# A four-layer attention and expert kernel: statistics taken where rows are made, a new order of matmuls in the second self attention

## The reference

```python
x = x + L0_xattn(ctx, layernorm(x), mask, ...)   # queries: x. keys: x and ctx. 8 heads of width 64
x = x + L0_ffn(layernorm(x), Wg, W1, W2)         # experts, one for each row
x = x + L1_xattn(layernorm(x), ctx, ctx, ...)    # 16 heads, softmax over 77 context rows, with wo
x = x + L1_ffn(layernorm(x), ...)                # self attention with 16 heads of 16, then 8 experts, 2 a row
x = x + L2_xattn(layernorm(x), ctx, pair_mask)   # 16 heads, relu squared over its sum, with wo
x = x + L2_ffn(layernorm(x), ...)                # 8 experts, 2 a row
x = x + L3_xattn(layernorm(x), ctx, ...)         # 16 heads, softmax, no wo
x = x + L3_ffn(layernorm(x), ...)                # fp4 rounded gate, up and down
```

```python
scores = einsum('bqhd,bkhd->bhqk', q, k) / sqrt(16)      # 2 x 16 heads x 1024 x 1024
o = einsum('bhqk,bkhd->bqhd', softmax(scores), v)
```

## Time and profile before

| | |
|---|---|
| median of 3 runs | 2685.7 us (2677.44 to 2688.1) |
| the profiled execution | 2695.88 us, its span 2694.1 us |
| PE busy with matmuls | 2201.1 us (82%) |
| PE busy with weight loads | 1304.1 us (48%) |
| DVE | 1298.8 us (48%) |
| ACT | 1087.3 us (40%) |
| POOL | 651.7 us (24%) |
| moved by DMA | 214.34 MB, mean 80 GB/s |
| instructions | 36343 |

### The profile page before, as it was taken

How to read it: one execution, slowest core, us unless ns; L and a number is a source line. 1 busy time by engine, 2 the same in 40 slices (tenths; PEclk the granted TensorE clock), 3 DMA queues, 4 the chain that set the end, 5 groups by cost and what they waited for, 6 DMA issues and landing times. The chain is left out here.

```text
span 2694.1 us, 36343 instructions
## 1 busy us (share of the span) xinstructions
PE 2201.1 (82%) x12198; PEld 1304.1 (48%) x12199; DVE 1298.8 (48%) x2560; ACT 1087.3 (40%) x2189; POOL 651.7 (24%) x569
## 2 busy tenths in 40 slices
PE   5899999953948766999998399994976999767786
PEld 2333333242933431333333299994345999633454
DVE  5655555165154557578871600004452350164785
ACT  3434444420314511566666244442532444325111
POOL 1238888911520050000000022220001222110011
PEclk9899999985977885699999699997887999978898
DMA  2000000022610053223420665652036666400000
GB/s 64 5 1 13 13 10 13 25 67 91 203 59 1 20 148 40 32 32 45 51 33 1 190 214 195 199 191 89 1 118 233 198 201 203 138 13 1 0 1 32
DMA packets 141630, 214.34 MB, mean 80 GB/s; under 512 B 39600, under 2 KB 97644, under 8 KB 141500
## 3 DMA queue, kind: packets, MB, share of 16 engines
q1 hardware_dynamic: 131228, 186.10, 25.3%
q0 software_dynamic: 9696, 26.49, 2.6%
q10 hardware_dynamic: 576, 0.07, 0.0%
HBM read 182.00 MB, written 30.15 MB: 79 GB/s over the span
## 5 line engine op out<-in xcount | busy, mean ns | idle before, releaser
L1840 DVE TENSOR_REDUCE heads_part_max<-heads_shared_ps 128x2 f32<-128x1024 f32 x256 | 300.1, 1220 | 93.5 <-PE heads_shared_ps L1757 93.5
L1824 ACT ACTIVATE heads_probs<-heads_score_ps 128x512 f32<-128x512 f32 x512 | 266.4, 603 | 194.4 <-PE heads_score_ps L1779 194.4
L2873 PE MATMUL experts_up_ps<-experts_rowT,experts_w 128*128 128x128 f32 x2864 | 342.9, 279 | 0.0
L2873 PEld LDWEIGHTS experts_up_ps<-experts_rowT,experts_w 128*128 128x128 f32 x2864 | 334.9, 195 | 0.2
L3033 DVE TENSOR_TENSOR experts_y<-experts_down_ps,experts_b_now 128x256 f32<-128x256 f32 x78 | 33.1, 425 | 499.5 <-PE experts_down_ps L2883 499.3
L1354 POOL TENSOR_TENSOR core_xT<-core_xT,heads_probs 128x1024 f32<-128x1024 f32 (+1 forms) x112 | 264.4, 2360 | 24.0 <-ACT heads_probs L1527 10.5
L2941 ACT ACTIVATE experts_hT<-experts_up_ps,experts_b_now 128x128 f32<-128x128 f32 x624 | 222.8, 367 | 49.0 <-PE experts_up_ps L2873 11.8
L1566 DVE TENSOR_REDUCE heads_part_max<-heads_shared_ps 128x1 f32<-128x512 f32 x256 | 164.5, 686 | 146.7 <-PE heads_shared_ps L1396 146.5
L1779 PE MATMUL heads_score_ps<-heads_q,heads_k 66*128 66x512 f32 x512 | 199.4, 478 | 29.2 <-ACT heads_probs L1824 24.9
L2822 POOL DMA_INDIRECT y_dram<-experts_y,experts_index x101 | 99.4, 984 | 456.3 <-DVE experts_y L3033 412.0
L1527 ACT ACTIVATE heads_probs<-heads_score_ps 128x1024 f32<-128x1024 f32 x128 | 131.0, 1023 | 177.8 <-PE heads_score_ps L1423 177.8
(11 more groups left out here) (557 smaller groups left out, 3242.7 us busy)
## 6 DMA issues: line engine op xcount, KB each, us to landing
experts_w<-in_L_ffn_W SPq DMA_DIRECT2D x39, 1024.0 KB, 5.2
experts_w<-in_L_ffn_w SPq DMA_DIRECT2D x39, 1024.0 KB, 5.0
experts_w<-in_L_ffn_W SPq DMA_DIRECT2D x23, 512.0 KB, 4.0
experts_w<-y_dram SPq DMA_DIRECT2D x20, 512.0 KB, 4.7
experts_b_now<-in_L_ffn_b SPq DMA_DIRECT2D x78, 128.0 KB, 2.9
heads_q<-l_queries SPq DMA_DIRECT2D x32, 256.0 KB, 11.9
heads_k<-l_keys SPq DMA_DIRECT2D x32, 256.0 KB, 13.6
l1f_w<-in_L_ffn_W SPq DMA_DIRECT2D x8, 1024.0 KB, 10.6
```

Source lines behind the costliest of these rows:

```text
L1824: act.activation(probs[:, t % SLOTS_OF_PROBS, r, :], score_ps[:, i % RING, :], ACT.Exp, scale=SC).then_inc(exp_done, 1)
L1840: dve.tensor_reduce(part_max[:, g % 2, 2 * pair:2 * pair + 2, s, x], two, AX.X, ALU.max).then_inc(shared_read, 1)
L2873: done = pe.matmul(up_ps[:, f % 4, 0:SLOT], w1_sb[:, u, c, f * P:(f + 1) * P], rowT[:, u % 2, c, :], start=(c == 0), stop=(c == DC - 1))
```

## The change

Three things change.

1. **Statistics.** `core.stats` is a new buffer of the whole program (128 x 16 x 6). Whoever makes rows also takes their `bn_stats` into it: the load (now in four DMAs of four tiles, with a semaphore each), the last adds of heads0, x1, x2, x3 and out1, and the combine of the experts. `layer_norm` no longer takes any. It works in one piece of 16 tiles, not in two of eight, and ACT takes the root of one column (`warm`) ahead of all else in the stage. The rows of the experts come back into four buffers (in the space of `w1`, as before), so SP no longer waits for `combined` between them.
2. **Queries** of x1 and x3: the four matmuls for `m + 2` stand behind jobs 1, 2, 3 and 4 of `m`, one each, not all behind job 7.
3. **Second self attention.** The fourth score of a step stands behind the step's two peak items, not before them. And `keep_running(n)` is new: n full matmuls of 512 columns, whose result nobody reads, 18 ahead of step 0, and one behind each of the first three scores and of each peak item in steps 0 and 1 (10 more).

The core of the diff:

```diff
+        self.stats = stage.sb("stats", [P, NT, 6])
...
-            sp.dma_start(core.x[:], x.rearrange("b (t p) d -> p (b t) d", p=P)).then_inc(x_loaded, 16)
-            sp.wait_ge(x_loaded, 16)
+            for u in range(NT // FOUR):
+                sp.dma_start(core.x[:, FOUR * u:FOUR * (u + 1), :], tiles[:, FOUR * u:FOUR * (u + 1), :]
+                             ).then_inc(x_loaded[u], 16)
...
+            for t in range(NT):
+                if t % FOUR == 0:
+                    dve.wait_ge(x_loaded[t // FOUR], 16)
+                dve.bn_stats(core.stats[:, t, :], core.x[:, t, :]).then_inc(counted, 1)
...
-            def statistics(t):
-                dve.bn_stats(stats[:, t, :], source[:, t, :]).then_inc(stats_done, 1)
...
             dve.memset(eps[:], LN_EPS).then_inc(eps_done, 1)
-            for t in range(PER):
-                statistics(t)
...
+            done(dve.tensor_tensor(diff[:], stats[:, :, 1], stats[:, :, 4], ALU.subtract))
+            done(dve.tensor_tensor(var[:], stats[:, :, 2], stats[:, :, 5], ALU.add))
+            done(dve.tensor_tensor(mean[:], stats[:, :, 1], stats[:, :, 4], ALU.add))
...
+            dve.wait_ge(std_done, 1)
+            done(dve.reciprocal(rstd[:], std[:]))
...
+            for t in range(NT):
                 normalise(t)
...
+            act.activation(warm[:], eps[:], ACT.Sqrt).then_inc(warmed, 1)
+            act.wait_ge(var_done, 1)
+            act.activation(std[:], var[:], ACT.Sqrt, scale=1.0 / D, bias=eps[:, 0:1]).then_inc(std_done, 1)
...
                     for job in range(8 * m, 8 * (m + 1)):
                         peak(job)
-                    if m + 2 < T // 512:
-                        queries(m + 2)
+                        x = job - 8 * m
+                        if m + 2 < T // 512 and 1 <= x <= DC * DC:
+                            query(m + 2, (x - 1) // DC, (x - 1) % DC)
...
                     dve.tensor_tensor(rows, rows, heads_out[:, part, :, :], ALU.add).then_inc(added, 1)
+                    if g == DC - 1:
+                        dve.wait_ge(added, part + 1)
+                        for t in range(b * BT, (b + 1) * BT):
+                            dve.bn_stats(core.stats[:, t, :], core.x[:, t, :]).then_inc(counted, 1)
...
+                for t in range(g * GROUP, (g + 1) * GROUP):
+                    dve.wait_ge(finished, t + 1)
+                    dve.bn_stats(core.stats[:, t, :], core.x[:, t, :]).then_inc(counted, 1)
...
+        BEFORE, EARLY = 18, 2
...
+            def keep_running(times):
+                for _ in range(times):
+                    pe.matmul(sums_ps[:], q_narrow[:, 0, 0:P], q_narrow[:, 0, 0:512], start=True,
+                              stop=True).then_inc(rested, 1)
+
             for item in work_at[-1]:
                 share(item)
+            keep_running(BEFORE)
             for t in range(STEPS):
                 items = work_at[t]
-                for r in range(QUAD):
+                early = t < EARLY
+                for r in range(QUAD - 1):
                     score(t, r)
+                    if early:
+                        keep_running(1)
                 for item in items[0:2]:
                     share(item)
+                    if early:
+                        keep_running(1)
+                score(t, QUAD - 1)
+                if t == 1:
+                    pe.wait_ge(rested, BEFORE + EARLY * (QUAD + 1))
                 if t:
                     value(t - 1)
...
             for x in range(NT // TILES):
-                if x >= 2:
-                    sp.wait_ge(combined, TILES * K * (x - 1))
                 for k in range(K):
...
-                    sp.dma_start(back[:, x % 2, k, :, :], y_dram[first:first + TILES * P, :].rearrange(
-                        "(t p) d -> p t d", p=P)).then_inc(returned[x % 2], 16)
+                    sp.dma_start(back[:, x, k, :, :], y_dram[first:first + TILES * P, :].rearrange(
+                        "(t p) d -> p t d", p=P)).then_inc(returned[x], 16)
...
+                for y in range(TILES):
+                    t = x * TILES + y
+                    dve.wait_ge(combined, TILES * (K * (x + 1) - 1) + y + 1)
+                    dve.bn_stats(core.stats[:, t, :], core.x[:, t, :]).then_inc(counted, 1)
```

135 lines of the change are left out of this document (57 added, 78 removed).

## The result

The changed kernel took 2606.97 us (median of 4 runs, 2598.55 to 2609.01); the kernel before, on the same chip, 2686.9 us (4 runs). The ratio is 0.9703, with an interval of 0.9671 to 0.9735. The forecast was 2610, a ratio of 0.972, in a range of 2585 to 2642. The profiled execution of the changed kernel took 2606.4 us with a span of 2604.7; the one of before had 2694.1. That one stood about 9 us above its kernel's median, the one after at its median.

The account below looks back on a forecast made before the run. No one engine bounds the kernel: handover holes and a falling TensorE clock do. Norms with producers -29, clock -22, order -15, queries -11 sum to -77, taken as -76: 2695.9 to 2620 profiled, 2610 us as median; range 2585 to 2642.

Parts of the forecast that it names:

- Norms (-44.7): Nine layer norms: delay from first statistic to first normalised row falls from 62.6 to 20.4 us; with smaller gains, 44.7 less.
- Producers (+16): Stages that make rows pay for the statistics where DVE has no slack: combines, first self attention, x1 to x3, load; 15.8 us.
- the four buffers: Combines of sparse rows: loads all out at once land ahead, so DVE bounds; this pays a part of the statistics.
- Clock (-22): Second self attention: full matmuls raise the clock before the first score; first fifteen steps 67.8 to 43.6 us, start 2.2 later.
- the loop of DVE and two buffers: Second self attention: second peak pair needs the buffer freed by the previous step's second reduce, giving a 2.75 us step.
- the step that this would give: Second self attention: if the score waits for the whole drain and its weights, step some 2.81 us, order part -9.
- a clock that rises no earlier: Rival, second self attention: full matmuls do not raise the clock earlier; +2 in place of -22, 2634 us; chance 0.12.
- 15 x 0.45 us: Second self attention, in that rival: got back from the order over 15 steps, of 0.55 us the fourth score waits.
- Queries (-11): x1 and x3: query matmuls spread over jobs 1 to 4 make a round 8.1 us against 11.5; 11 us less.
- The lower end of the range, -25: Whole kernel: the parts' bounds taken as independent give some -25 and +32, with the first three rivals within 2585 to 2642.
- the parts' bounds: Whole kernel: margins about -6/+11 (norms and producers), -4/+24 (clock), -11/+15 (order), -2/+9 (queries) us.
- two signs of being wrong: Second self attention: steps of 4 us past the first and steps above 2.85 us would show the forecast wrong.

## Why the prediction was right, point by point

**Norms (-44.7): right**, -47.9. The first hats came at 1.46, 1.95 and 3.2 us against 1.45, 2.15 and 3.35. None waited for anything else, and no stage behind gave it back.

**Producers (+16): right**, about +16 by the stages (load 1.9, heads0 3.1, gates and experts 7.9, x3 3.5 in the run with the statistics alone). The combines cost +6.7 of +8.1, the load +1.9, the last 2.71 us of x3's statistics stand behind its last sum (forecast 2.8):

```profile
2396.71 1.23 DVE L784 TENSOR_TENSOR core_x<-core_x,x_heads_out 128x1024 f32<-128x1024 f32 x1
2397.97 2.71 DVE L788 BATCH_NORM_STATS2 core_stats<-core_x 128x6 f32<-128x256 f32 x8
```

What the text said of the four buffers, that they pay a part of the statistics, was wrong: they pay nothing. With statistics between the sums, the loads land in time in two buffers as well.

**Clock (-22): right in size**. Steps 0 to 14 took 43.5 us against 67.8 (forecast 43.6), and the first score came 1.7 us later behind the first peak item (51.5 against 49.8; forecast 2.2): -22.6. What no row had shown, how soon the clock answers, is 1.9 to 4.9 us.

**Order (-15): right in size and in mechanism**, -17.3 (41.6 less 24.3). The step was to be 2.75 in the mean by the loop of DVE and two buffers, and is 2.64 and 2.85 in turn; with less of DVE's work it falls to 2.64 and no lower, against the 2.66 forecast for a step without that loop. The Trainium skill (TensorEngine Tiling (Array Packing), Key Properties) has it that a change of the tiling mode drains TensorE; the step that this would give was put at 2.81. In the changed kernel the fourth change stands where PE used to wait, and the step is 2.64 where DVE does not hold it, 0.03 over the 2.61 of a step without peaks. The rule is not refuted by that: with PE full and one change more (the second item behind the values), a step took 0.31 more, of which some 0.10 are left for the change, close to the 0.12 of the prediction.

**Where a step of the text failed.** For a clock that rises no earlier the text got 15 x 0.45 us back from the order, 2634 in all. It took the 0.55 us in the row of PEld for a wait of PE; PE waited 0.03 us a step, and the order gave nothing at 1.2 GHz (4.71 a step against 4.62). With the full matmuls taken away the clock rose at step 19, later than in any profile with the old order (7, 13 and 15). That the median then stood at 2638.8, near 2634, is no support for that term: by the text the order alone would take 22 us off the steps (15 and 7), and it took 8.2. The same misreading stands in the case for that rival, that PE waited 0.55 us of each step and the clock stayed down all the same: it stayed down without even that wait. The forecast came out because order and full matmuls went together.

**Queries (-11): the mechanism right, the size somewhat too large.** x1's and x3's maxima took 29.8 us each, 6.1 and 4.1 less, near the forecast. At the stages' ends some 9 us were left over all profiles with the statistics, 7 by the changed kernel's own, and alone 2 in the medians (not to be told from none), since the stretches at 1.2 GHz move when anything ahead of them moves, and a query with its job takes 2.63 us there in place of 1.43.

**Range and signs.** The lower end of the range, -25, does not follow from the parts' bounds: taken as independent (the root of the sum of squares, which gives the +32 above) they give -13, 2597, and the measured 2607 lies inside that too. By the letter two signs of being wrong were there, a second step of 4.02 us, with its five full matmuls in it (forecast 3.4), and steps above 2.85, those with a copy, a turn or a group's end. The latter were longer before (the two steps behind a group's end took 4.18 and 2.92 us, now 3.49 and 3.17), so neither speaks against the mechanism.

The sum fits also by luck. The rows of the two profiled executions differ by 89.4 us, 12 more than forecast: norms and order gave 5 us more, and x2 8 us, of which nothing was forecast. The text carried the 10 us by which the profile of before stood above its median over to the changed kernel, whose profile stands at its median; the two nearly cancel, and the median came out 3 us from the forecast. That x2 at 1.2 GHz was most of those 10 is likely and not shown.

**Left open:** why the clock rises at step 7, 13 or 15 in the old order and at 19 in both runs of the new order without full matmuls. Two runs against three don't show that the order is the cause. In both of the two it rose within the first fold, eight transposes of 128 by 128 in a row, 1.2 and 1.3 us after the row's start (at 1144.26 with the order alone, at 1123.58 without the full matmuls); with the old order it rose among ordinary rows, before any fold. The row with the order alone:

```profile
1143.04 1.67 PE L1766 MATMUL heads_shared_ps<-core_ident,heads_sums 128*128 128x128 f32 x8
```

So the fold may have ended it, and without one the clock may have stayed down longer; no run tests that. What keeps x2 at 2.4 GHz in some profiles is open as well.

## What to carry to other kernels

Put statistics where rows are made, and look at the barrier behind as the price list: everything between it and the first useful row is paid by all engines. Where a stage starts at the lower clock behind a wait, fill the wait with full matmuls in a row; and do this before a change that takes PE's waits away, for where the lower clock already keeps PE busy throughout there is no wait to take. Read a wait from the row of the engine that is the path: an idle PEld is not an idle PE. When two profiles differ in a stage that was not edited, look at its granted clock before looking for a cause.

## What the runs showed of the hardware

- A PE that is busy for 84.86 of 85 us (scores over 66 rows, peaks over 32 rows and values into 32 columns, these two four at a time) stayed at 1.2 GHz; full bfloat16 matmuls of 128 rows and 512 columns in a row lifted the clock 1.9 to 4.9 us after the first.
- The same stage of 566 matmuls took 111.6 to 121.5 us, by how much of it ran at 1.2 GHz.
- A row of two peak items between scores takes PE 0.32 us at 2.4 GHz, and so does a single one: on different 32 rows they run side by side. Split, they cost a full step 0.31 us more.
- ACT's table load of 1.28 us starts with the stage when a root without a wait stands first, which takes 0.86 us off the way to the first hat.
